# One bias product less for each batch, degrees by reductions, and another order on GpSimd, in a graph network with LSTM windows

## The chip, the cores and the metric

The kernel runs on one core of a Trainium2 chip. The metric is the device time of the launch in microseconds, the median of three runs. Profiles give one execution.

## The reference, cut to what matters

Sixteen batches b of a 512x128 matrix x, and one 512x512 matrix adj for all of them:

```
h = relu(layernorm(x))
h = relu(adj @ (h @ Wg0 + bg0))
h = relu(adj @ (h @ Wg1 + bg1))
for p in 1..4:                        # windows of p tokens
    h[:, p-1::p] = last hidden state of LSTM p over each window of p tokens
x = x + h
h = relu(layernorm(x))
A = adj + I
deg = sum(A, axis=0) + sum(A, axis=1) - diag(A)
A_hat = A * deg[:,None]**-0.5 * deg[None,:]**-0.5
z = relu(batchnorm((A_hat @ h) @ W1.T + b1));  z = batchnorm(z @ W2.T + b2)
out = x + z
```

Both batch norms take their statistics over all batches and tokens.

## The kernel before, in words

Features lie on the partitions, the 512 tokens of a batch in the free axis. Each matrix product in fp32 accuracy is made as three products of split operands (hi x hi, hi x lo, lo x hi, lines 1093 to 1095). The hi part of a tile is a copy by ScalarE in the type fp32r, and the lo part, what is left, is made by VectorE (lines 754 and 756), for some LSTM inputs by GpSimd (line 390). So each step of the first layers runs through TensorE (into a PSUM bank), ScalarE (hi) and VectorE (lo).

The first two layers of a batch are four units. AGG0 multiplies the normed x by adj. LIN0 multiplies by Wg0; since adj @ (h @ Wg0 + bg0) = (adj @ h) @ Wg0 + rowsum(adj) x bg0, it first puts the outer product of bg0 and the row sums of adj into the bank (line 1149, 512 columns), and ScalarE makes h1 by a relu that reads the bank (line 597). It has no lo part. LIN1 (lines 1152 and 1154) reads h1, AGG1 multiplies by adj again.

The main loop has four rounds of 22 slots. A slot is one step of an LSTM on one of two chains: slots 0 to 3 are p = 1, 4 to 7 p = 2, 8 to 13 p = 3, 14 to 21 p = 4. TensorE makes the gates into one of six banks, ScalarE the sigmoids and tanhs (line 641, three instructions; the tanh of the cell at line 651), VectorE the cell and state (lines 925 to 957). Beside it run, by fixed slot numbers, the units of the next four batches (PRE_POS: LIN0 at slots 1, 10, 14 and 19, LIN1 one slot later) and the second network of the batches of the round before (POST_POS). The units of the first four batches stand in the prologue, in an order written out by hand (PROLOGUE), between the banks of weights that are transposed and split. Every engine walks the same lists and works in order. For VectorE a slot is: the LSTM step, then the units' lo parts, then statistics and norms, then what belongs to the matrix A_hat. For ScalarE the relu of LIN0 comes ahead of the next slot's gates.

GpSimd makes in each slot the norms (line 361 to 371) that are due, and the lo parts that the following steps of p = 3 and p = 4 read (line 390).

A_hat is made in round 0. DEG_SUM (slot 3) is 16 products on TensorE that sum rows and columns of adj over all partitions (lines 1201, 1203, 1205), less the diagonal, which VectorE takes out in the prologue (lines 831 and 836). VectorE then takes the partition's own entry out (line 885) and sums (line 889), GpSimd takes the power -0.5 (slot 4, line 405), VectorE builds diagonal blocks of it (DINV_DIAG, slot 5, line 895), TensorE spreads them (DINV_ROWS, slot 7), and VectorE makes four chunks of A_hat (HAT_CHUNK, slots 8, 11, 14, 17; lines 867 to 876 and a lo part).

Of the kernel before, what the change touches and what calls it, by code (L numbers as in the profile page):

```python
# [139 lines left out]
def build(nc, x, adj, Wg0, bg0, Wg1, bg1, Wih, Whh, bih, bhh, W1, b1, g1, be1, W2, b2, g2, be2, out):  # L140
# [7 lines left out]
    with whole:  # L148
# [22 lines left out]
        bg0_row = sb("bg0_row", [P, P], F32R)  # L171
        rowsum_row = sb("rowsum_row", [P, T], F32R)
# [7 lines left out]
        deg = sb("deg", [P, CHUNKS])  # L180
# [57 lines left out]
        def f32(ap):  # L238
# [12 lines left out]
        fix_part, fix_ready, deg_mm, deg_part, deg_ready = (  # L251
            sem("fix_part"), sem("fix_ready"), sem("deg_mm"), sem("deg_part"), sem("deg_ready"))
# [9 lines left out]
        pre_mm, pre_hi, pre_lo, h1_ready = sem("pre_mm"), sem("pre_hi"), sem("pre_lo"), sem("h1_ready")  # L262
# [81 lines left out]
        def _(pool):  # L344
# [8 lines left out]
            nc.gpsimd.memset(f32(bg0_row[:, :]), 0.0)  # L353
# [31 lines left out]

            def later_class(r, chain, q, c):
# [5 lines left out]
            for slot in range(N_SLOTS):  # L392
# [3 lines left out]
                for kind, n in PRE_AFTER[slot]:  # L396
                    if kind == "stats":
                        norm_pre(n)
                for kind, n in POST_AFTER[slot]:
                    if kind == "stats":  # L400
                        norm_post(n, y_post)
                if slot == DEG_POW:

                    pool.wait_ge(deg_ready, 1)
                    nc.gpsimd.tensor_tensor(dinv[:, :], deg[:, :], minus_half[:, :], ALU.pow).then_inc(dinv_ready, 1)
# [947 lines left out]
```

## Time and profile before

| what | value |
|---|---|
| median of three runs | 567.07 us (564.61 to 568.53) |
| the profiled execution | 565.18 us, its span 563.4 us |
| mean granted clock of TensorE | 0.973 of full speed |
| busy: TensorE, VectorE, ScalarE, GpSimd | 90%, 73%, 63%, 35% of the span |
| the chain of work that ended last: TensorE, issue, VectorE, GpSimd, ScalarE | 49%, 21%, 12%, 9%, 5% |

The busy share is an average over the prologue (to about 51 us), four rounds (to about 480 us) and the two batch norms at the end. The timeline gives for each instruction its start and length, and in brackets the time for which its engine was idle before it and what released it. A mean granted clock under 1 in a stretch says that TensorE ran part of it at 1.2 and not at 2.4 GHz.

### The profile page before, as it was taken

How to read it: one execution, taken by the hardware profiler on the slowest of the kernel's cores; microseconds unless marked ns; L12 is line 12 of the kernel's file. 1: busy time of each engine (PE TensorE's matmuls, PEld its weight loads, DVE VectorE, ACT ScalarE, POOL GpSimd, SP SyncE). 2: the span in 40 equal slices, each digit the busy share in tenths (PEclk: the TensorE clock that was granted, in tenths of full speed). 3: DMA queues.
4: the chain of work that ended last, by engine and by line, in shares of the span. 5: the costliest groups of instructions: out<-in, count | busy, mean ns of one | idle time of the engine just before them, and what ended most of it. 6: DMA issues, size and time to landing. Idle time of an engine off the chain costs nothing.

```text
span 563.4 us, 7993 instructions
## 1 busy us (share of the span) xinstructions
PE 504.7 (90%) x2697; PEld 430.3 (76%) x2697; DVE 413.8 (73%) x957; ACT 353.2 (63%) x679; POOL 197.3 (35%) x299
## 2 busy tenths in 40 slices
PE   3998998797898999999989999999779998895866
PEld 3787787797897789988977889889557998673546
DVE  3646667788857888678578887775786888877867
ACT  3544765555567667566676575675766677456863
POOL 4502021304400647055005471440052514247940
PEclk9998999798999999999999999999999999997997
DMA  7300030000001011102011101010910000600007
GB/s 224 114 19 2 0 94 19 2 19 1 19 20 58 37 38 56 58 1 75 31 65 56 37 38 57 2 56 1 366 64 19 20 2 19 224 1 0 1 1 298
DMA packets 17837, 31.21 MB, mean 55 GB/s; under 512 B 1498, under 2 KB 6020, under 8 KB 17796
## 3 DMA queue, kind: packets, MB, share of 16 engines
q1 hardware_dynamic: 16804, 30.17, 15.7%
q10 hardware_dynamic: 992, 0.52, 0.4%
q8 instruction: 21, 0.34, 0.3%
q14 instruction: 20, 0.16, 0.1%
HBM read 19.16 MB, written 11.53 MB: 54 GB/s over the span
## 4 chain that ended last, share of the span: by engine, by line
PE 49%; issue 21%; DVE 12%; POOL 9%; ACT 5%; POOLq 3%; DMA 1%; DVEq 0%; ACTq 0%
PE gate_ps L1093 10%; PE gate_ps L1095 9%; PE gate_ps L1094 9%; PE pre_ps L1094 3%; PE pre_ps L1095 3%; PE pre_ps L1093 3%; POOL x_pre L371 3%; PE post_ps L1093 3%; POOL z_back L426 3%; PE post_ps L1095 2%; PE post_ps L1094 2%; POOLq L369 2%; ACT gate L651 2%; DVE cell L935 1%; PE pre_ps L1154 1%
## 5 line engine op out<-in xcount | busy, mean ns | idle before, releaser
L641 ACT ACTIVATE gate<-gate_ps,gate_bias 128x256 f32<-128x256 f32 (+2 forms) x312 | 164.0, 562 | 45.4 <-PE gate_ps L1095 43.8
L1093 PE MATMUL gate_ps<-by_class_hi,wih_hi 128*128 128x256 f32 (+2 forms) x264 | 86.5, 328 | 15.3 <-POOL by_class_lo L390 9.2
L651 ACT ACTIVATE gate<-cell 128x512 f32<-128x512 f32 (+2 forms) x88 | 45.3, 515 | 68.5 <-DVE cell L930 34.8
L1095 PE MATMUL gate_ps<-by_class_lo,wih_hi 128*128 128x256 f32 (+2 forms) x264 | 84.5, 320 | 0.0
L1094 PE MATMUL gate_ps<-by_class_hi,wih_lo 128*128 128x256 f32 (+2 forms) x264 | 84.4, 320 | 0.0
L1093 PEld LDWEIGHTS gate_ps<-by_class_hi,wih_hi 128*128 128x128 f32 x264 | 50.7, 192 | 22.9 <-POOL by_class_lo L390 10.7
L1093 PE MATMUL gate_ps<-hstep_hi,whh_hi 128*128 128x256 f32 (+2 forms) x192 | 60.7, 316 | 0.0
L1095 PE MATMUL gate_ps<-hstep_lo,whh_hi 128*128 128x256 f32 (+2 forms) x192 | 60.5, 315 | 0.0
L1094 PE MATMUL gate_ps<-hstep_hi,whh_lo 128*128 128x256 f32 (+2 forms) x192 | 60.5, 315 | 0.0
L390 POOL TENSOR_TENSOR by_class_lo<-h,by_class_hi 128x256 fp32r<-128x256 f32 (+1 forms) x40 | 36.8, 927 | 55.4 <-ACT by_class_hi L649 55.3
L1094 PEld LDWEIGHTS gate_ps<-by_class_hi,wih_lo 128*128 128x128 f32 x264 | 50.8, 192 | 3.5
L361 POOL TENSOR_TENSOR ln_pre<-mv_pre,eps 128x4 f32<-128x4 f32 x16 | 5.0, 314 | 137.5 <-DVE mv_pre L802 137.5
L1095 PEld LDWEIGHTS gate_ps<-by_class_lo,wih_hi 128*128 128x128 f32 x264 | 50.6, 192 | 2.3
L361 POOL TENSOR_TENSOR ln_post<-mv_post,eps 128x4 f32<-128x4 f32 x16 | 6.4, 403 | 130.4 <-DVE mv_post L802 130.4
L940 DVE TENSOR_TENSOR gate<-gate 128x256 f32<-128x256 f32 (+2 forms) x48 | 27.3, 569 | 26.3 <-ACT gate L651 26.3
L1094 PEld LDWEIGHTS gate_ps<-hstep_hi,whh_lo 128*128 128x128 f32 x192 | 37.2, 194 | 1.3
L1093 PEld LDWEIGHTS gate_ps<-hstep_hi,whh_hi 128*128 128x128 f32 x192 | 37.1, 193 | 1.3
L1095 PEld LDWEIGHTS gate_ps<-hstep_lo,whh_hi 128*128 128x128 f32 x192 | 37.0, 193 | 1.3
L371 POOL TENSOR_SCALAR x_pre<-x_pre,ln_pre 128x128 f32<-128x128 f32 x64 | 34.9, 557 | 2.8 <-issue 2.8
L371 POOL TENSOR_SCALAR y_post<-x,ln_post 128x128 f32<-128x128 f32 x52 | 33.5, 655 | 2.3 <-issue 2.3
L927 DVE TENSOR_TENSOR gate<-gate 128x256 f32<-128x256 f32 (+2 forms) x48 | 24.3, 506 | 12.5 <-ACT gate L641 12.3
L935 DVE TENSOR_TENSOR cell<-gate 128x512 f32<-128x512 f32 (+2 forms) x40 | 25.6, 640 | 7.3 <-ACT gate L641 7.1
(295 smaller groups left out, 1304.3 us busy)
## 6 DMA issues: line engine op xcount, KB each, us to landing
x_pre<-in_x SPq DMA_DIRECT2D x16, 256.0 KB, 2.7
x<-in_x SPq DMA_DIRECT2D x16, 256.0 KB, 2.7
z_spill<-z_ring SPq DMA_DIRECT2D x8, 512.0 KB, 2.7
z_back<-z_spill SPq DMA_DIRECT2D x8, 512.0 KB, 6.7
x_spill<-x SPq DMA_DIRECT2D x12, 256.0 KB, 2.0
x_back<-x_spill SPq DMA_DIRECT2D x1, 3072.0 KB, 11.2
out<-x_back SPq DMA_DIRECT2D x12, 256.0 KB, 2.3
x<-in_adj SPq DMA_DIRECT2D x1, 1024.0 KB, 6.4
```

Of the source, the lines that this page charges most:

```text
L361: nc.gpsimd.tensor_tensor(ln[:, 0, :], mv[:, :, 1], eps[:, :], ALU.add)
L371: last = nc.gpsimd.tensor_scalar(y[:, c * P:(c + 1) * P], src[:, c * P:(c + 1) * P], ln[:, 2, c:c + 1], ln[:, 1, c:c + 1], ALU.add, ALU.mult)
L390: nc.gpsimd.tensor_tensor(lo, states, f32(hi), ALU.subtract).then_inc(later_lo, 1)
L426: nc.gpsimd.tensor_scalar(zz, zz, bn1[:, 4, half:half + 1], bn1[:, 5, half:half + 1], ALU.mult, ALU.add).then_inc(t_pool, 1)
L641: nc.scalar.activation(gate[:, tile_of(g), gt, 0:size], gate_ps[k % GATE_BANKS][:, 0:size], ACT.Tanh if gt == G_GATE else ACT.Sigmoid, bia ...
L651: nc.scalar.activation(gate[:, tile_of(g), G_GATE, 0:size], cell[:, tile_of(g), 0:size], ACT.Tanh)\
L927: nc.vector.tensor_tensor(i_, i_, g_, ALU.mult).then_inc(ig_done, 1)
L935: nc.vector.tensor_tensor(c_, i_, g_, ALU.mult).then_inc(cell_ready, 1)
L940: nc.vector.tensor_tensor(i_, o_, g_, ALU.mult).then_inc(h_done, 1)
L1093: nc.tensor.matmul(ps, w[0], m[0], start=start, stop=False)
L1094: nc.tensor.matmul(ps, w[1], m[0], start=False, stop=False)
L1095: return nc.tensor.matmul(ps, w[0], m[1], start=False, stop=stop)
```

## The change

**The bias of LIN0.** The outer product at line 1149 is left out. In the prologue a 512-column matrix bias0 is made once: ScalarE copies the row sums of adj, which a bank holds on all partitions, and VectorE multiplies them by bg0, one value to a partition. For every batch VectorE adds bias0 to the bank and writes h1 (both inputs are read with a step of four elements, h1 is written densely); ScalarE then makes the relu in place in h1. There are sixteen such adds, four of them in the prologue.

**The degrees.** The 16 products of slot 3, their two followers on VectorE and one of the two diagonal operations leave. VectorE makes four reductions in the prologue: the rows of adj (in the raw matrix), the hi and the lo part of the transposed adj, and the diagonal. So that a partition holds the same tokens in both, adj is loaded with four consecutive rows to a partition, and the transposes write every fourth column. GpSimd adds the four sums and takes the power ahead of the main loop. DINV_DIAG moves from slot 5 to 2, DINV_ROWS from 7 to 4, the chunks from slots 8, 11, 14, 17 to 5, 9, 12, 17. SyncE's loads of x1 wait for the reductions and not for the products.

**GpSimd's order.** In a slot whose successor makes lo parts, the norms due in it are made one slot later on GpSimd, behind those lo parts. The prologue's second statistics also move behind bank 0 and the first norm.

```diff
-DEG_SUM, DEG_TOKENS, DEG_POW, DINV_DIAG, DINV_ROWS = 3, 3, 4, 5, 7
-HAT_CHUNK = (8, 11, 14, 17)
+DINV_DIAG, DINV_ROWS = 2, 4
+HAT_CHUNK = (5, 9, 12, 17)
+def makes_parts(slot):
+    return slot < N_SLOTS and TURNS[slot][2] >= 3 and TURNS[slot][3] + 1 < TURNS[slot][2]
+NORMS_AFTER = [[at for at in (slot - 1, slot) if at >= 0 and makes_parts(at + 1) == (at < slot)] for slot in range(N_SLOTS)]
...
 PROLOGUE
-        [("stats", 0), ("stats", 1), ("bank", 0), ("norm", 0), ...
+        [("stats", 0), ("bank", 0), ("norm", 0), ("stats", 1), ...
...
-                     ("bank", 7), (LIN1, 0), (LIN1, 1), (LIN0, 2), ("bank", 8), (AGG0, 3), (AGG1, 0), ("bank", 9),
-                     (LIN0, 3), (LIN1, 2), (AGG1, 1), ("bank", 10)]
+                     ("bank", 7), (LIN1, 0), (LIN1, 1), (LIN0, 2), ("bank", 8), ("deg", DEG_ROWS), (AGG0, 3), ("deg", DEG_HI), (AGG1, 0), ("bank", 9),
+                     (LIN0, 3), (LIN1, 2), ("deg", DEG_LO), (AGG1, 1), ("bank", 10)]
...
-                    + [(LIN1, 3), ("bank", 11), (AGG1, 2), ("bank", 12)]
+                    + [(LIN1, 3), ("bank", 11), ("deg", DEG_DIAG), (AGG1, 2), ("bank", 12)]
...
 GpSimd
+            pool.wait_ge(deg_ready, 4)
+            nc.gpsimd.tensor_tensor(deg[:, DEG_ROWS, :], deg[:, DEG_ROWS, :], deg[:, DEG_HI, :], ALU.add)
...
+            nc.gpsimd.tensor_tensor(dinv[:, :], deg[:, DEG_ROWS, :], minus_half[:, :], ALU.pow).then_inc(dinv_ready, 1)
...
+                for at in NORMS_AFTER[slot]:
+                    for kind, n in PRE_AFTER[at]:
...
 SyncE
-            sp.dma_start(adj_raw[:, :, :], adj.rearrange("(c p) s -> p c s", p=P)).then_inc(adj_in, 16)
+            sp.dma_start(adj_raw[:, :, :], adj.rearrange("(p c) s -> p c s", c=CHUNKS)).then_inc(adj_in, 16)
...
-                    sp.wait_ge(deg_mm, 1)
+                    sp.wait_ge(deg_ready, 4)
...
 ScalarE
-                    last = nc.scalar.activation(rowsum_row[:, :], ps[:, :], ACT.Copy)
+                    last = nc.scalar.activation(bias0[:, :], ps[:, :], ACT.Copy)
...
+                if k == LIN0:
+                    act.wait_ge(h1_sum, b + 1)
+                    nc.scalar.activation(h1[i][:, :, :], h1[i][:, :, :], ACT.Relu).then_inc(h1_ready, 1)
+                    return
                 act.wait_ge(pre_mm, q + 1)
-                if k == LIN0:
-                    nc.scalar.activation(h1[i][:, :, :], ps[:, :].rearrange("h (p c) -> h c p", c=CHUNKS), ACT.Relu)\
...
 VectorE
+                    last = nc.vector.tensor_scalar(bias0[:, :], bias0[:, :], bg0_col[:, 0:1], None, ALU.mult)
...
+                if k == LIN0:
...
+                    dve.wait_ge(pre_mm, pre_number(b, k) + 1)
+                    nc.vector.tensor_tensor(h1[i][:, :, :], ps[:, :].rearrange("h (p c) -> h c p", c=CHUNKS),
+                                            bias0[:, :].rearrange("h (p c) -> h c p", c=CHUNKS), ALU.add).then_inc(h1_sum, 1)
+                    return
...
+            def deg_part(i):
+                if i == DEG_DIAG:
...
+                        last = nc.vector.tensor_tensor(deg_fix[:, c, :], adj_raw[:, c, c::CHUNKS], ident[:, :], ALU.mult)
...
+                src = {DEG_ROWS: adj_raw, DEG_HI: adj_t[0], DEG_LO: adj_t[1], DEG_DIAG: deg_fix}[i][:, :, :]
...
+                nc.vector.reduce_sum(deg[:, i, :], src, AX.X).then_inc(deg_ready, 1)
...
 TensorE
-                        last = nc.tensor.transpose(ps[:, c * P:(c + 1) * P], adj_raw[:, c, i::CHUNKS], ident[:, :])
+                        last = nc.tensor.transpose(ps[:, c::CHUNKS], adj_raw[:, c, i::CHUNKS], ident[:, :])
...
-                    nc.tensor.matmul(ps[:, :], bg0_row[:, :], rowsum_row[:, :], start=True, stop=False)
-                    last = product(ps[:, :], [part[:, :] for part in wg0], [part[:, :] for part in agg[i]], False, True)
+                    last = product(ps[:, :], [part[:, :] for part in wg0], [part[:, :] for part in agg[i]], True, True)
...
-                if n == DEG_SUM:
-                    for c in range(CHUNKS):
-                        nc.tensor.matmul(post_ps[:, :], ones_f[:, :], adj_raw[:, c, :], start=c == 0, stop=False)
-                        for part in adj_t:
-                            nc.tensor.matmul(post_ps[:, :], ones_r[:, :], part[:, c, :], start=False, stop=False)
...
```

How VectorE's instructions stand in the prologue, before, around the lo part of the third aggregated batch (agg_lo) and the second linear unit's u_lo:

```order
L756 TENSOR_TENSOR wih_lo<-gate_ps,wih_hi 128x512
L756 TENSOR_TENSOR agg_lo<-gate_ps,agg_hi 128x512
L754 SCALAR_TENSOR_TENSOR lstm_in_lo<-pre_ps,lstm_in_hi 128x512
L756 TENSOR_TENSOR wih_lo<-gate_ps,wih_hi 128x512
L756 TENSOR_TENSOR u_0_lo<-gate_ps,u_0_hi 128x512
```

And the same place in the changed kernel:

```order
L837 TENSOR_TENSOR h_0<-gate_ps,bias 128x512
L771 TENSOR_TENSOR wih_lo<-gate_ps,wih_hi 128x512
L859 TENSOR_REDUCE deg<-x 128x4
L771 TENSOR_TENSOR agg_lo<-gate_ps,agg_hi 128x512
L859 TENSOR_REDUCE deg<-adj_t_hi 128x4
L769 SCALAR_TENSOR_TENSOR lstm_in_lo<-pre_ps,lstm_in_hi 128x512
L771 TENSOR_TENSOR wih_lo<-gate_ps,wih_hi 128x512
L837 TENSOR_TENSOR h_1<-gate_ps,bias 128x512
L771 TENSOR_TENSOR u_0_lo<-gate_ps,u_0_hi 128x512
L859 TENSOR_REDUCE deg<-adj_t_lo 128x4
```

Two adds of bias0 (h_0 and h_1) and three reductions stand between the lo parts that were neighbours.

VectorE in slot 1 of round 0, before (two state products of p = 1, then the hi and lo part of the state), and what follows is the next slot:

```order
L935 TENSOR_TENSOR cell<-gate 128x512
L948 TENSOR_TENSOR cell<-gate 128x512
L950 CAST by_class_hi<-cell 128x512
L756 TENSOR_TENSOR by_class_lo<-cell,by_class_hi 128x512
L935 TENSOR_TENSOR cell<-gate 128x512
```

The same slot in the changed kernel:

```order
L952 TENSOR_TENSOR cell<-gate 128x512
L965 TENSOR_TENSOR cell<-gate 128x512
L967 CAST by_class_hi<-cell 128x512
L771 TENSOR_TENSOR by_class_lo<-cell,by_class_hi 128x512
L837 TENSOR_TENSOR h_0<-pre_ps,bias 128x512
L952 TENSOR_TENSOR cell<-gate 128x512
```

The add stands behind the slot's lo part. On ScalarE the relu of h_0 keeps its place, between the tanh (line 666) and the even tokens (line 675), and reads h_0 where it read the bank.

GpSimd around slots 6 to 9 of round 0, before: the norm of a batch (lines 361 to 371) and the lo parts for p = 3.

```order
L361 TENSOR_TENSOR ln_pre<-mv_pre,eps 128x4
L362 TENSOR_TENSOR ln_pre<-mv_pre,minus_one 128x4
L364 TENSOR_TENSOR ln_pre<-ln_pre,minus_half 128x4
L371 TENSOR_SCALAR x_pre<-x_pre,ln_pre 128x128 x4
L390 TENSOR_TENSOR by_class_lo<-h,by_class_hi 128x340 x4
```

The same place in the changed kernel:

```order
L409 TENSOR_TENSOR by_class_lo<-h,by_class_hi 128x340
L369 TENSOR_TENSOR ln_pre<-mv_pre,eps 128x4
L370 TENSOR_TENSOR ln_pre<-mv_pre,minus_one 128x4
L372 TENSOR_TENSOR ln_pre<-ln_pre,minus_half 128x4
L379 TENSOR_SCALAR x_pre<-x_pre,ln_pre 128x128 x4
L409 TENSOR_TENSOR by_class_lo<-h,by_class_hi 128x340 x3
```

The first of the four lo parts now stands ahead of the norm.

## Rows read from the trace of the kernel before

**Rows 1.** The page: busy us, share of the span and instruction counts of each engine.

```profile
PE 504.7 (90%) x2697; PEld 430.3 (76%) x2697; DVE 413.8 (73%) x957; ACT 353.2 (63%) x679; POOL 197.3 (35%) x299
```

**Rows 2.** Busy by stretch: PE, PEld, DVE, ACT, POOL; PEclk, DMA, GB/s.

```profile
12.00:51.00 39.00, 36.63 (x189) 30.04 (x189) 23.31 (x62) 19.55 (x46) 12.91 (x26) 1.00 0.22 62
66.00:72.40 6.40, 6.40 (x27) 4.05 (x26) 4.68 (x8) 3.77 (x7) 0.00 (x0) 1.00 0.00 0
97.00:103.00 6.00, 1.11 (x5) 0.83 (x5) 5.24 (x10) 2.67 (x6) 5.68 (x9) 0.74 0.00 0
...
181.00:277.00 96.00, 93.84 (x533) 83.02 (x534) 74.41 (x190) 62.44 (x128) 44.23 (x66) 1.00 0.12 42
```

**Rows 3.** Timeline: start us, us, engine, line, op, tiles, shapes, count, idle before.

```profile
102.17 0.65 PE L1093 MATMUL gate_ps<-by_class_hi,wih_hi 128*128 128x340 f32 x1 [4.89 <-POOL by_class_lo L390]
...
134.62 0.58 PE L1093 MATMUL gate_ps<-by_class_hi,wih_hi 128*128 128x256 f32 x1 [2.38 <-POOL by_class_lo L390]
...
469.15 0.38 PE L1093 MATMUL gate_ps<-by_class_hi,wih_hi 128*128 128x256 f32 x1 [1.91 <-POOL by_class_lo L390]
```

**Rows 4.** The chain that ended last, round 1: start us, us, what.

```profile
171.39 1.33 ACT gate L641 x2
...
181.88 0.23 PE gate_ps L1093
```

**Rows 5.** VectorE's groups by shape: busy us, mean ns, then idle before.

```profile
L754 DVE SCALAR_TENSOR_TENSOR hid_lo<-z_back,hid_hi 128x1024 fp32r<-128x1024 f32 x9 | 11.2, 1247 | 3.5 <-ACT hid_hi L733 3.5
...
L870 DVE TENSOR_TENSOR z_ring<-z_ring,ident 128x128 f32<-128x128 f32 x4 | 1.8, 440 | 0.1
```

**Rows 6.** Timeline, slots 1 and 2 of round 0.

```profile
62.57 0.67 ACT L660 ACTIVATE h<-cell 128x256 f32<-128x256 f32 x1 [0.27 <-DVE cell L948]
...
63.04 0.69 DVE L756 TENSOR_TENSOR by_class_lo<-cell,by_class_hi 128x512 fp32r<-128x512 f32 x1
63.05 1.80 ACT L641 ACTIVATE gate<-gate_ps,gate_bias 128x512 f32<-128x512 f32 x3
```

**Rows 7.** Timeline, round 0, slots 3 to 6.

```profile
72.66 0.88 DVE L885 TENSOR_TENSOR z_ring<-post_ps,ident 128x128 f32<-128x128 f32 x4 [1.11 <-PE post_ps L1205]
...
73.34 2.07 ACT L641 ACTIVATE gate<-gate_ps,gate_bias 128x512 f32<-128x512 f32 x3 [2.29 <-PE gate_ps L1095]
...
85.47 0.88 DVE L895 TENSOR_SCALAR z_ring<-ident,dinv 128x128 f32<-128x128 f32 x4 [2.19 <-POOL dinv L405]
```

**Rows 8.** Timeline of the prologue, VectorE and TensorE.

```profile
33.97 0.69 DVE L756 TENSOR_TENSOR agg_lo<-gate_ps,agg_hi 128x512 fp32r<-128x512 f32 x1 [2.00 <-ACT agg_hi L601]
...
51.54 0.50 PE L1093 MATMUL gate_ps<-lstm_in_hi,wih_hi 128*128 128x512 f32 x1 [1.87 <-DVE w_lo L756]
```

**Rows 9.** Timeline, slots 8 to 11 of round 0.

```profile
98.67 0.51 DVE L756 TENSOR_TENSOR hstep_lo<-gate,hstep_hi 128x340 fp32r<-128x340 f32 x1
...
99.70 0.77 DVE L867 TENSOR_TENSOR z_ring<-adj_t_hi,adj_t_lo 128x512 f32<-128x512 f32 x1
...
103.65 0.50 DVE L935 TENSOR_TENSOR cell<-gate 128x340 f32<-128x340 f32 x1
...
106.05 0.51 DVE L925 TENSOR_TENSOR cell<-gate,cell 128x340 f32<-128x340 f32 x1
...
111.45 0.68 DVE L754 SCALAR_TENSOR_TENSOR nrm_lo<-x_pre,nrm_hi 128x512 fp32r<-128x512 f32 x1
...
112.72 0.40 PE L1152 MATMUL pre_ps<-bg_row,ones_r 128*128 128x512 f32 x1
```

**Rows 10.** Timeline, round 0, slots 14 and 19.

```profile
130.23 0.58 ACT L597 ACTIVATE h<-pre_ps 128x512 f32<-128x512 f32 x1
...
131.49 0.68 DVE L867 TENSOR_TENSOR z_ring<-adj_t_hi,adj_t_lo 128x512 f32<-128x512 f32 x1
...
157.89 0.42 DVE L925 TENSOR_TENSOR cell<-gate,cell 128x256 f32<-128x256 f32 x1
...
158.49 0.39 PE L1152 MATMUL pre_ps<-bg_row,ones_r 128*128 128x512 f32 x1
```

More of the change, by code:

```diff
@@ L395, in _ @@
                     later_class(r, chain, p, step + 1)
[L396 to L405, printed above, removed]
+                for at in NORMS_AFTER[slot]:
+                    for kind, n in PRE_AFTER[at]:
+                        if kind == "stats":
+                            norm_pre(n)
+                    for kind, n in POST_AFTER[at]:
+                        if kind == "stats":
+                            norm_post(n, y_post)
             for n in range(LATE, LATE + 2):
@@ L552, in rows_hi_parts @@
                     nc.scalar.activation(wg1[:, :], wg_raw[:, 1, :], ACT.Copy).then_inc(wg_hi, 1)
+                else:
                     act.wait_ge(bias_in, 32)
-                    for row in (0, 32, 64):
-                        last = nc.scalar.activation(bg0_row[row:row + 1, :], bias_rows[row:row + 1, 0, :], ACT.Copy)
-                else:
                     for row in (0, 32):
@@ L560, in rows_hi_parts @@
                                                         bias_rows[row:row + 1, 1, :], ACT.Copy)
-                last.then_inc(rows_hi, 1)
+                    last.then_inc(rows_hi, 1)
             def bank_hi(k):
@@ L769, in rows_lo_parts @@
                         last = low(part, bias_rows[32:33, 1, :], part)
-                last.then_inc(rows_ready, 1)
+                    last.then_inc(rows_ready, 1)
             def bank_lo(k):
@@ L821, in pre_unit @@
                 low(dst[1], src, dst[0], relu=func == ACT.Relu).then_inc(pre_lo, 1)
+            def deg_part(i):
+                if i == DEG_DIAG:
+                    dve.wait_ge(consts_ready, 3)
+                    for c in range(CHUNKS):
+                        last = nc.vector.tensor_tensor(deg_fix[:, c, :], adj_raw[:, c, c::CHUNKS], ident[:, :], ALU.mult)
+                    last.then_inc(diag_part, 1)
+                    dve.wait_ge(diag_part, 1)
+                if i == DEG_HI:
+                    dve.wait_ge(setup_hi, CHUNKS)
+                if i == DEG_LO:
+                    dve.wait_ge(setup_lo, CHUNKS)
+                src = {DEG_ROWS: adj_raw, DEG_HI: adj_t[0], DEG_LO: adj_t[1], DEG_DIAG: deg_fix}[i][:, :, :]
+                if i in (DEG_HI, DEG_LO):
+                    src = f32(src)
+                nc.vector.reduce_sum(deg[:, i, :], src, AX.X).then_inc(deg_ready, 1)
             for kind, i in PROLOGUE:
@@ L825, in _ @@
                     bank_lo(i)
[L826 to L838 removed]
+                elif kind == "deg":
+                    deg_part(i)
                 elif kind == "rows":
@@ L1164, in _ @@
                     bank(i)
-                elif kind not in ("stats", "norm", "rows"):
+                elif kind not in ("stats", "norm", "rows", "deg"):
                     if kind == LIN0 and i == 0:
-                        pe.wait_ge(setup_lo, CHUNKS + 1)
                         pe.wait_ge(wg_ready, 1)
+                    if kind == LIN1 and i == 0:
                         pe.wait_ge(rows_ready, 1)
-                    if kind == LIN1 and i == 0:
-                        pe.wait_ge(rows_ready, 2)
                     pre_unit(kind, i, prologue_ps(i), i % 2)
```

71 lines of the change are left out of this document (24 added, 47 removed).

## The prediction

> **What bounds the kernel now.** I read the page first, then the busy time by stretch, then the chain that ended last, then the timeline around each place that the change touches. The page makes TensorE the fullest engine, 90% busy, and VectorE the next with 73% [rows 1]. The stretches say where that holds [rows 2]: in the round from 181 to 277 us TensorE computes 93.84 of 96 us, but in the prologue (12 to 51 us) it has 2.4 us to spare and VectorE 15.7 us. The timeline has three places at which TensorE idles for a lo part that GpSimd makes, 4.89 + 2.38 + 1.91 = 9.2 us in all [rows 3]. The chain shows that in the four short slots that open a round (p = 1) the limit is not TensorE's products but the alternation of ScalarE's gates and VectorE's state products; rows 4 hold the first such piece of round 1 and the TensorE piece with which it ends. So there are three regimes: TensorE in the middle of a round, the chain of ScalarE and VectorE at its start, and a prologue in which the engines hand each other tiles.
>
> The sum is made against the profiled execution, 565.2 us (its span is 563.4). It lies 1.9 us under the median of the three runs, 567.07.
>
> **Prices.** A 512-column product costs TensorE 0.23 us [rows 4]. The bias product of the first linear layer is one such; there are sixteen. The new add of VectorE reads a PSUM tile and the kept matrix, 128x512 each, both with neighbours 16 bytes apart, and writes h1 densely. The nearest row with that step in SBUF is the identity added to every fourth column: 440 ns for 128 elements, on average [rows 5]. The four products that read PSUM at that step took 0.88 us [rows 7], 0.22 each, so the step in PSUM costs nothing. The identity's add runs partly beside GpSimd, so of its excess of 0.22 over those I give the step about half, 0.12 us per 128 elements. It has the step on its read and on its write, the new add on one SBUF read. A dense 128x512 operation of VectorE takes 0.69 us [rows 6]. The ends are therefore 0.69 and 0.69 + 4 x 0.12 = 1.17, and I take the middle, 0.93, as one of the two steps is there. The relu in place I take at its old 0.58 [rows 10].
>
> The Trainium skill, "SBUF — State Buffer", Door 1, says that accesses keep the full rate only while at least two fall on each 16-byte line, and that PSUM's lines are 8 bytes, so that non-contiguous PSUM patterns slow matmuls. By the first half the add would cost the upper end, and the sum below would be 1.9 us higher. By the second half the adjacency transposes, which now write every fourth column, would be slower than before; the dense price of rows 7 for a PSUM read at that step does not show it, and no row here shows it for that transpose.
>
> A reduction over 2048 elements: I count it by what it reads, as a dense operation of VectorE: 512 take 0.69 [rows 6], 1024 take 1.25 [rows 5], so 0.56 for each further 512 and 2.4 in all. Three of them are 7.1, the diagonal 0.88 + 0.69 = 1.6, the four adds of the prologue 3.7, less 0.3 for a bias row: 12.1 us on a VectorE with 15.7 idle.
>
> **Prologue: +3.1.** VectorE's idle time comes in pieces of 2.0 us, each before a tile that TensorE wants next [rows 8]. Walking the new order: the relu of batch 0 stands ahead of nrm_hi of batch 2 on ScalarE and now waits for VectorE's add; that delays the third aggregation by about 1.2 (0.93, and what stands ahead of the add). Reductions of 2.4 us in gaps of 2.0 leave 0.4 each, 1.2. The diagonal block stands near the end, where nothing hides it, 1.6. Against them stand four bias products, 0.9. 1.2 + 1.2 + 1.6 - 0.9 = 3.1. Ends: -0.9, if all is hidden, and +6.0, if half of the 12.1 is exposed. Stats of batch 1 behind the first lo parts let aggregation 0 start sooner, but aggregation 1 waits for batch 1 as before: nothing.
>
> **Slot 1 of round 0: +2.7.** VectorE's state tail comes first in its queue and the add behind it. The lo part starts at 63.04 and frees the engine 0.61 later, the add takes 0.93, the relu 0.58: h1 is ready at 65.2 [rows 6]. ScalarE waits in order: its even tokens come behind the relu, the gates of slot 2 another 0.48 on (62.57 to 63.05), at 65.7 and not at 63.05, 2.65 later.
>
> **Slots 2 to 8: -1.4.** The degree products fill TensorE for 6.3 of the 6.4 us from 66.0 [rows 2]. What that costs the chain is ScalarE's wait before the next gates, 2.29 us at 73.34 [rows 7]. Without the products ScalarE and VectorE set the pace, so I count 2.3 and not 6.3. DINV_DIAG moves to slot 2 and puts 0.9 on the same chain. Its old wait and itself, 2.19 + 0.88 = 3.1 [rows 7], are replaced by the first hat chunk, which is 4.0 beside GpSimd [rows 9] and which I put at 3.1 without it: even. -2.3 + 0.9 = -1.4.
>
> **Slots 8 to 11: -1.6.** Before 102.17 the lo part waits behind a norm. Taken first it is ready before 97, and the hidden state decides: 98.67 + 0.51 = 99.18, a gain of 3.0 [rows 3, 9]. The granted clock is 0.74 from 97 to 103, so part of that stretch at 1.2 GHz [rows 2], and the product behind the pause takes 0.65 us for 340 columns [rows 3], where 512 take 0.39 at 158.49 [rows 10]. Six such at 0.3 too much are 1.8. Some two microseconds of idling remain, so I credit half, 0.9. But the second hat chunk moves from slot 11 to slot 9, ahead of slot 10's states, and takes 4.0 (99.70 to 103.65). Those states and their tail take 5.4 (106.05 to 111.45), of which 2.0 are waits that the chunk uses up [rows 9]. So VectorE is through slot 9 at 106.05 - 3.9 = 102.15, through the chunk at 106.1, through slot 10 at 109.5, and add and relu end at 111.1, where TensorE asked for h1 at 112.72: 1.6 is left of the 3.9.
>
> **Slots 14 and 19 of round 0: +0.7.** The wait of 2.38 at 134.62 goes [rows 3], but the add can start only at the end of VectorE's tail, 131.49, so the relu ends at 133.00 and not at 130.81; TensorE ran until 132.24, 1.43 behind the relu, and would until 134.4: -0.2. At slot 19 the tail ends at 157.89, the relu at 159.40, and TensorE asks at 158.49 [rows 10]: +0.9. The three bias products of slots 10 to 19 gain nothing here, as TensorE waits.
>
> **Rounds 1 and 2: +3.9.** Slot 1 lies on the chain that ends at 181.88 [rows 4]: +2.65 each. At slots 10, 14 and 19 a slot's products stand between relu and use on a TensorE that is full there [rows 2], so I count no wait; three bias products leave it, -0.7 in each round. 2 x 1.95 = 3.9.
>
> **Round 3: -1.9**, the third wait for GpSimd [rows 3].
>
> Sum: 3.1 + 2.7 - 1.4 - 1.6 + 0.7 + 3.9 - 1.9 = +5.5, and 565.2 + 5.5 = 570.7. GpSimd's norms start up to 1 us later; ScalarE wants them two slots on, nothing. The x loads start earlier behind the degrees, nothing. The adjacency's longer rows lie between -1 and 0; I take 0.
>
> **The rivals.** *TensorE is the bound everywhere.* Then the degree products count in full (6.3), so do sixteen bias products (3.7), the waits for GpSimd down to their next input (3.0, nearly all of 2.38, and 1.91: 6.8 with 1.9 for the second) and the half-rate products (1.8): -18.6, 547; if half is given back at the relu, 556. For it: 93.84 of 96 us. Against it: rows 7, where the neighbour waited only 2.29, and rows 4. Chance of less than 561.4: 0.25. The Trainium skill, "Perfetto Trace Analysis", Identifying the Most-Contended Engine, says to optimise the engine of highest occupancy first; by that rule this rival would be the outcome.
>
> *VectorE has no gap left before the main loop.* Place: the lo parts behind the reductions. If half of the 12.1 us is exposed the prologue costs 6.0 and not 3.1, and an add of 1.17 puts 0.24 on eight exposed places, 1.9: 570.7 + 2.9 + 1.9 = 575.5. It decides once the prologue costs 5.1, or as soon as it costs 3.2 with that add. For it: gaps of 2.0 for pieces of 2.4. Against it: 15.7 us idle. Chance of more than 572.7: 0.33.
>
> *GpSimd's new order does nothing*, since another input is as late: the gains of 1.6, 0.2 and 1.9 fall away, 574.4, and its chance, 0.05, is within the 0.33.
>
> **How the numbers follow.** A measurement of this kernel tells about 1%, 5.7 us, from no change. The forecast lies 3.6 above the median, within it: same 0.42, slower 0.33, faster 0.25. The range from 557 to 578 leaves out 2 in 10: the full gain of TensorE below, a wholly exposed prologue above. The likeliest case alone spans 565 to 573.
>
> **What would show it.** The first gate product moves from 51.54 [rows 8] to about 54.6. The adds last 0.93, the reductions 2.4. In slot 1 of every round ScalarE waits about 2 us for the add, and TensorE for h1 before the second linear layer. The wait at 73.34 is gone, and TensorE has new idle time between slots 4 and 6. No wait on GpSimd's lo part is left at 102 and 469. I am wrong if ScalarE's waits for the add are short, or if the first gate product starts at 51.5 or sooner.

## The result, and the profile after

| | before | changed |
|---|---|---|
| median | 567.04 us (564.61 to 568.53, 4 runs) | 578.67 us (577.85 to 580.92, 4 runs) |
| ratio | | 1.0213, 95% interval 1.0178 to 1.0247 |
| profiled execution, its span | 565.18, 563.4 us | 578.66, 576.9 us |
| mean granted clock | 0.973 | 0.967 |

The change costs 11.6 us, 2.1%. The forecast was 570.7, the range 557 to 578: the sign of the sum was right and the size was not, and the result lies outside. Between the two profiled executions the difference is 13.5 us.

The page of the changed kernel, which answers to [rows 1]: TensorE has lost 32 products (40 records, as each of the eight that read a plain f32 tile stands twice in the trace) and is by this count as busy as before; VectorE has 19.5 us more.

```profile
PE 505.0 (88%) x2657; PEld 428.7 (74%) x2657; DVE 433.3 (75%) x967; ACT 349.0 (60%) x676; POOL 191.3 (33%) x302
```

VectorE's new instructions, grouped by shape (busy us, mean ns, idle before); below, ScalarE's relu from the page, with the idle time ahead of it:

```profile
L837 DVE TENSOR_TENSOR h<-pre_ps,bias 128x512 f32<-128x512 f32 x13 | 13.7, 1054 | 0.0
...
L859 DVE TENSOR_REDUCE deg<-x 128x4 f32<-128x2048 f32 x1 | 2.3, 2275 | 0.0
```

```profile
L612 ACT ACTIVATE h<-h 128x512 f32<-128x512 f32 x16 | 10.1, 631 | 41.0 <-DVE h L837 41.0
```

The add takes 1.05 us (the sum had 0.93, ends 0.69 and 1.17), a reduction 2.28 (2.4), the relu in place 0.63 (0.58). The last row is the important one: in sixteen places ScalarE stood for 41.0 us in all before a relu, waiting for the add.

Slot 1 of round 0, timeline, which answers to [rows 6]:

```profile
65.11 0.69 DVE L771 TENSOR_TENSOR by_class_lo<-cell,by_class_hi 128x512 fp32r<-128x512 f32 x1
65.72 1.04 DVE L837 TENSOR_TENSOR h<-pre_ps,bias 128x512 f32<-128x512 f32 x1
66.79 0.63 ACT L612 ACTIVATE h<-h 128x512 f32<-128x512 f32 x1 [2.91 <-DVE h L837]
67.33 0.64 ACT L675 ACTIVATE h<-cell 128x256 f32<-128x256 f32 x1
67.48 0.54 PE L1167 MATMUL pre_ps<-bg_row,ones_r 128*128 128x512 f32 x1 [2.42 <-ACT h L612]
67.77 1.79 ACT L656 ACTIVATE gate<-gate_ps,gate_bias 128x512 f32<-128x512 f32 x3
```

Lo part, add, relu, even tokens and gates run one behind the other, as forecast. ScalarE waited 2.91 us, TensorE 2.42 for h1.

A simple way to place the loss is to take one event that each slot has, ScalarE's tanh of the cell (88 in a run), and to subtract its start before from its start after. By stretches, in us, for the profiled executions (the columns on the right belong to experiments below: without the bias part; with the add moved):

| stretch, to the tanh of | forecast | changed | without bias | add early |
|---|---|---|---|---|
| prologue, slot 0 | +3.1 | +2.5 | -2.0 | +4.0 |
| slots 1 and 2 | +2.7 | +2.2 | -0.4 | 0.0 |
| slots 3 to 8 | -1.4 | -2.1 | -2.1 | -2.1 |
| slots 9 to 21 of round 0 | -0.9 | +1.2 | -6.6 | -5.2 |
| rounds 1 and 2 | +3.9 | +7.5 | +0.4 | -0.7 |
| round 3 | -1.9 | +2.4 | +2.6 | +1.2 |
| sum | +5.5 | +13.8 | -8.1 | -2.8 |

Up to the end of round 0 the forecast holds in sum (+3.5 against +3.8). It is lost in rounds 1 and 2 (3.6) and in round 3 (4.3). In rounds 1 and 2 the step behind slot 1 is +2.65 and +2.66; most of the rest comes at slot 10. There, in round 1, the changed kernel's timeline shows on VectorE and ScalarE:

```profile
225.54 0.47 ACT L666 ACTIVATE gate<-cell 128x340 f32<-128x340 f32 x1
226.04 0.96 DVE L957 TENSOR_TENSOR gate<-gate 128x340 f32<-128x340 f32 x1 [0.61 <-ACT gate L666]
...
227.87 1.07 DVE L837 TENSOR_TENSOR h<-pre_ps,bias 128x512 f32<-128x512 f32 x1
...
228.97 0.63 ACT L612 ACTIVATE h<-h 128x512 f32<-128x512 f32 x1 [2.96 <-DVE h L837]
...
230.60 1.84 ACT L656 ACTIVATE gate<-gate_ps,gate_bias 128x340 f32<-128x340 f32 x4
...
233.20 0.49 ACT L666 ACTIVATE gate<-cell 128x340 f32<-128x340 f32 x1 [0.35 <-DVE cell L947]
```

and the kernel before, at the same place, had

```profile
219.60 0.49 ACT L651 ACTIVATE gate<-cell 128x340 f32<-128x340 f32 x1 [0.47 <-DVE cell L930]
220.00 0.58 ACT L597 ACTIVATE h<-pre_ps 128x512 f32<-128x512 f32 x1
...
221.57 1.56 ACT L641 ACTIVATE gate<-gate_ps,gate_bias 128x340 f32<-128x340 f32 x3
...
224.36 0.49 ACT L651 ACTIVATE gate<-cell 128x340 f32<-128x340 f32 x1
```

Before, 4.76 us lie from tanh to tanh (219.60 to 224.36); now 7.66 (225.54 to 233.20). The add is behind VectorE's tail, the relu behind the add, and all of the next slot's gates stand behind the relu on ScalarE. TensorE, which I had looked at, goes on with gate products it has banks for and hardly waits; the chain of ScalarE and VectorE is what slips. Not all of the 2.9 us are the add's: without the bias part this step still grows by 0.6, and so it does with GpSimd's order alone. VectorE's product at 226.04 takes 0.96 beside a lo part of GpSimd, where it took 0.51 before. Of the 2.9 us 1.8 are made good in the two slots that follow, and slot 14 adds 0.8.

### The profile page after: what moved, and what is told of

The parts are those of the page before. It is cut to its first block, busy times and chain, and to the rows that moved or that the text cites. A ratio compares the mean times of both kernels' runs of the same rounds, so it can differ in the third digit from the quotient of the medians.

```text
span 576.9 us, 7923 instructions
## 1 busy us (share of the span) xinstructions
PE 505.0 (88%) x2657; PEld 428.7 (74%) x2657; DVE 433.3 (75%) x967; ACT 349.0 (60%) x676; POOL 191.3 (33%) x302
## 4 chain that ended last, share of the span: by engine, by line
PE 36%; DVE 31%; issue 12%; ACT 11%; POOL 6%; POOLq 2%; DVEq 1%; DMA 1%; ACTq 0%
PE gate_ps L1109 7%; PE gate_ps L1111 7%; PE gate_ps L1110 7%; ACT gate L666 4%; ACT gate L656 3%; POOL z_back L443 3%; PE pre_ps L1109 3%; DVE gate L957 2%; PE pre_ps L1111 2%; PE pre_ps L1110 2%; DVE cell L952 2%; DVE hstep_lo L771 2%; DVE cell L947 2%; PE post_ps L1109 2%; DVE gate L944 2%
## 5 line engine op out<-in xcount | busy, mean ns | idle before, releaser
L656 ACT ACTIVATE gate<-gate_ps,gate_bias 128x256 f32<-128x256 f32 (+2 forms) x312 | 160.8, 563 | 34.3 <-PE gate_ps L1111 32.8
L409 POOL TENSOR_TENSOR by_class_lo<-h,by_class_hi 128x256 fp32r<-128x256 f32 (+1 forms) x40 | 35.1, 877 | 160.6 <-ACT by_class_hi L664 160.6
L1109 PEld LDWEIGHTS gate_ps<-by_class_hi,wih_hi 128*128 128x128 f32 x264 | 51.2, 194 | 19.5 <-issue 11.5
L957 DVE TENSOR_TENSOR gate<-gate 128x256 f32<-128x256 f32 (+2 forms) x48 | 28.0, 584 | 26.5 <-ACT gate L666 26.5
L612 ACT ACTIVATE h<-h 128x512 f32<-128x512 f32 x16 | 10.1, 631 | 41.0 <-DVE h L837 41.0
L379 POOL TENSOR_SCALAR x_pre<-x_pre,ln_pre 128x128 f32<-128x128 f32 x64 | 33.5, 535 | 2.8 <-issue 2.8
L944 DVE TENSOR_TENSOR gate<-gate 128x256 f32<-128x256 f32 (+2 forms) x48 | 25.5, 531 | 9.8 <-ACT gate L656 9.7
L379 POOL TENSOR_SCALAR y_post<-x,ln_post 128x128 f32<-128x128 f32 x52 | 31.7, 621 | 2.3 <-issue 2.3
```

The lines of the kernel that those rows point to most:

```text
L379: last = nc.gpsimd.tensor_scalar(y[:, c * P:(c + 1) * P], src[:, c * P:(c + 1) * P], ln[:, 2, c:c + 1], ln[:, 1, c:c + 1], ALU.add, ALU.mult)
L409: nc.gpsimd.tensor_tensor(lo, states, f32(hi), ALU.subtract).then_inc(later_lo, 1)
L656: nc.scalar.activation(gate[:, tile_of(g), gt, 0:size], gate_ps[k % GATE_BANKS][:, 0:size], ACT.Tanh if gt == G_GATE else ACT.Sigmoid, bia ...
L944: nc.vector.tensor_tensor(i_, i_, g_, ALU.mult).then_inc(ig_done, 1)
L957: nc.vector.tensor_tensor(i_, o_, g_, ALU.mult).then_inc(h_done, 1)
L1109: nc.tensor.matmul(ps, w[0], m[0], start=start, stop=False)
```

## The experiments

Each was timed beside the kernel before on the same chip (566.5 to 566.9 us there).

### One part alone, and all but one

The four edits are: the bias part on the kernel before; the degrees part on it; GpSimd's order on it; and the changed kernel with the bias part taken back. For example the last:

```diff
-                    last = product(ps[:, :], [part[:, :] for part in wg0], [part[:, :] for part in agg[i]], True, True)
+                    nc.tensor.matmul(ps[:, :], bg0_row[:, :], rowsum_row[:, :], start=True, stop=False)
+                    last = product(ps[:, :], [part[:, :] for part in wg0], [part[:, :] for part in agg[i]], False, True)
```

> The kernel before with the bias part alone: VectorE adds the kept matrix, ScalarE makes the relu in place; degrees and GpSimd's order as before. If the add on the way to h1 is the cause, slot 1 of rounds 0 to 2 gives +2.65 each (8.0), slots 10, 14 and 19 some +1.5 in each round, and the prologue nothing or +1: 567 + 12 = 579. If the degree reductions carry the loss, this kernel loses at most half of the 11.6 us: 573 or less.

> The degrees part alone (reductions on VectorE in the prologue, hat chunks earlier, statistics of batch 1 later), bias product on TensorE and GpSimd's order as before. If the add is the cause: the prologue costs +2.5 and slot 4 gives 2.7 back, 567 within 2. If the reductions are the cause: 573 or more.

> GpSimd's order alone: lo parts ahead of the norms. In the changed kernel slot 9 of round 0 came 3.9 us sooner and lost it in slots 10 and 11 behind the add; without the add it should keep 2 to 3 us of it, and the waits at slot 14 of round 0 and slot 17 of round 3 give up to 1 each: 563 to 565. A rival: the later norms give it back, 567.

> The changed kernel with the bias product back on TensorE and the relu back on the bank; degrees on VectorE and GpSimd's new order stay. If the add is the cause: 562 to 566, at or under the kernel before. If the reductions are: 572 or more.

| kernel | us | ratio to before, 95% |
|---|---|---|
| bias alone | 582.95 | 1.0245 to 1.0321 |
| degrees alone | 565.75 | 0.994 to 1.000 |
| GpSimd's order alone | 566.47 | 0.9981 to 1.0015 |
| degrees and order, no bias | 558.28 | 0.9817 to 0.9884 |

The bias part is the whole loss: +16.4 us alone, and +20.4 on top of the other two, which without it are 8.2 us faster than the kernel before. My expectation for the bias alone (579) was 4 too low, and 562 to 566 for the kernel without it was 4 too high. The degrees alone came as expected (565.75 for 567 within 2). GpSimd's order alone was expected at 563 to 565 and gives nothing in the time. In its trace it gains 3.0 us in slots 9 to 21 of round 0 and gives back 0.9 in rounds 1 and 2 and 1.05 in round 3; what else its profile loses is 1.4 in the prologue, whose program is unchanged, and 1.6 at slots 6 and 7 of round 3, behind a fall of the granted clock.

Degrees and order together are worth far more than the two alone (-0.8 and 0). By slots, the two alone sum to +0.2 and together make -8.1. Of the 8.3 us, 4.5 lie in round 3, where the profiles of the single parts had falls of the granted clock (below), 2.3 in slots 9 to 21 of round 0, mostly at slot 16, where the kernel with the early chunks and GpSimd's old order loses 2.7 again (TensorE waits 2.35 for GpSimd's lo part at 130.24), and 1.6 in the prologue, which GpSimd's order does not touch: that much two profiles can differ for no reason. So the size of this interplay is measured, its parts are only placed.

### The add's place, its length, and the relu's place

Add moved ahead of VectorE's wait for the tanh, in slot 1 alone, or everywhere (then without the condition):

```diff
+                if p == 1:
+                    for kind, n in PRE_AFTER[g]:
+                        if kind == LIN0:
+                            pre_unit(kind, n, pre_ps, 0)
                 dve.wait_ge(tanh_ready, g + 1)
```

Kept matrix stored in h1's order:

```diff
-                    last = nc.scalar.activation(bias0[:, :], ps[:, :], ACT.Copy)
+                    last = nc.scalar.activation(bias0[:, :].rearrange("h (c p) -> h c p", c=CHUNKS),
+                                                ps[:, :].rearrange("h (p c) -> h c p", c=CHUNKS), ACT.Copy)
```

For the late relu, the call moves on ScalarE from the end of slot g to behind the gates of slot g + 1.

> The changed kernel with the add of slot 1 moved on VectorE: behind the cell's product and ahead of the wait for the tanh, where VectorE idles 0.7 us. If the 2.65 us per round are the add's place behind the state's tail, slot 1 costs at most 0.6 and three rounds give back 6: 572.5. If they are the longer way itself (add and relu one behind the other, wherever they stand), 577 or more.

> The changed kernel with the kept matrix stored in h1's order, so that the add reads it densely and only the bank with a step. If the step in SBUF makes the add 1.05 us and not 0.69, the add falls to 0.7 and, on 10 to 13 exposed places, the kernel to 574.5. If the step in PSUM is what costs, the add stays at 1.05 and the time at 578.

> The changed kernel with ScalarE's relu of LIN0 behind the next slot's gates, not ahead of them: ScalarE no longer stands before the add, TensorE still waits for h1 before the second linear layer. If ScalarE's wait in its queue is the cost, slots 1 and 10 give back most of what they lose: 568 to 572. If TensorE's wait for h1 is, the time stays at 577 or more, as the relu comes still later.

> The changed kernel with the add ahead of the wait for the tanh in every slot that has one, the kept matrix read with its step as before (1.05 us). Moved in slot 1 alone it gave 6 us, moved everywhere and dense 18.5. If slots 10, 14 and 19 lose by the add's place, this kernel comes to 563 to 565; if the shorter add is what mends them, to 570.

> The changed kernel with both mendings: the dense kept matrix (3 us) and the add ahead of the wait for the tanh, in slots 10, 14 and 19 too. The slot-1 move gave 6 us; in the other slots the add now delays the state by up to 0.4 but lets the relu end some 0.9 sooner. Sum 578.7 - 3 - 6 - 1 = 569. If the longer slots suffer from the delayed state, 572.

| kernel | us | against the changed kernel |
|---|---|---|
| add early in slot 1 | 572.65 | -6.0 |
| add early in every slot | 561.78 | -16.9 |
| dense kept matrix | 575.6 | -3.1 |
| add early everywhere, and dense | 560.18 | -18.5 |
| relu late | 585.17 | +6.5 |

The add's place is the cause. Early, it uses the time in which VectorE waits for the tanh; timeline of slot 1 of round 0 with the add early in slot 1:

```profile
63.43 0.69 DVE L952 TENSOR_TENSOR cell<-gate 128x512 f32<-128x512 f32 x1 [0.89 <-ACT gate L656]
64.04 1.07 DVE L837 TENSOR_TENSOR h<-pre_ps,bias 128x512 f32<-128x512 f32 x1
64.16 0.63 ACT L666 ACTIVATE gate<-cell 128x512 f32<-128x512 f32 x1 [0.18 <-DVE cell L952]
65.02 0.69 DVE L969 TENSOR_TENSOR cell<-gate 128x512 f32<-128x512 f32 x1
65.14 0.63 ACT L612 ACTIVATE h<-h 128x512 f32<-128x512 f32 x1 [0.35 <-DVE h L837]
```

The add delays the state's product by 0.2 us, ScalarE waits 0.35 instead of 2.91. In slot 10 of round 1, with the add early everywhere, the relu follows the tanh after 0.43 of idling:

```profile
215.78 1.08 DVE L837 TENSOR_TENSOR h<-pre_ps,bias 128x512 f32<-128x512 f32 x1
...
215.96 0.50 ACT L666 ACTIVATE gate<-cell 128x340 f32<-128x340 f32 x1
...
216.90 0.64 ACT L612 ACTIVATE h<-h 128x512 f32<-128x512 f32 x1 [0.43 <-DVE h L837]
```

With the add early everywhere ScalarE's waits for it sum to 16.1 us, not 41.0. Against my doubt about the longer slots, the moved place helped there too: slots 10, 14 and 19 were worth 10.9 us beside slot 1's 6.0. Against the kernel with slot 1 alone moved, the tanh behind slot 10 comes 2.0 to 2.4 us sooner in each round and the one behind slot 14 1.3 to 1.6; the one behind slot 19 comes 1.7 sooner in round 0 and no sooner in rounds 1 and 2, where the changed kernel had lost nothing there. The late relu was the wrong remedy: ScalarE's waits for the adds fell from 41.0 to 12.1 us, but TensorE's waits for h1 rose from 13.5 to 21.2. Against what was expected, the two single mendings came out (572.65 for 572.5, 575.6 for 574.5), the add early everywhere did better (561.78 for 563 to 565; with the dense matrix, which was run first, 560.18 for 569), and the late relu did the opposite (585.17 for 568 to 572).

The length counts less. One row of the kernel with the dense matrix (ns min/median/max, first and last start):

```profile
L838 DVE TENSOR_TENSOR h<-pre_ps,bias x13: 681/683/685, 20.3 to 390.8; 128x512 f32<-128x512 f32 x13
```

0.683 us instead of 1.05, although the bank is still read at a step of four. So the step in PSUM costs VectorE nothing, and the one step in SBUF costs 0.37 us for 512 elements, where the sum had taken 0.24. The Trainium skill, "SBUF — State Buffer", Door 1, says that full rate needs two accesses to each 16-byte line; the read that falls on one element of each is this case, and the trace agrees: 1.05 against 0.683. The same page's sentence on PSUM concerns matmuls, and the transposes that now write every fourth column took 417 ns at the median before and 418 after; no slowing shows.

### The prologue

The first four batches without bg0 (the add left out and the relu back on the bank; this part of the computation is missing), and, without the bias part, the second statistics back in front. Then the whole computation, with the bias of the first four batches on TensorE and of the other twelve by the early, dense add:

```diff
+                if k == LIN0 and b < EARLY:
+                    return
                 if k == LIN0:
```

> The changed kernel without bg0 for the first four batches (their relu reads the bank again, the add is left out; a part of the computation is missing). Before the main loop the changed kernel stood 4.5 us behind the kernel without the bias part. If these are the four adds of the prologue on a VectorE that the reductions have filled, it gives back about 4: 574.5. If they come from the reductions themselves, 578.

> The kernel without the bias part and with the old chunk slots, with the prologue's second statistics back in front of bank 0. That kernel reached the first slot 1.9 us sooner than the kernel before, in spite of 9 us of reductions. If the statistics' new place gives this, 559; if the reductions simply lie in VectorE's idle time and the diagonal operation that is gone gives it, 557.4.

> Bias product and relu from the bank for the first four batches, the dense add ahead of the tanh for the other twelve. The prologue's adds cost 4 us (574.8 without them against 578.7), less 1 for the second set of bias rows: 560.2 - 3 = 557. A rival: the added copies of the row sums take it back, 559.

Measured 574.8, 558.5 and 558.03 us. The first gate product of the changed kernel starts at

```profile
55.24 0.50 PE L1109 MATMUL gate_ps<-lstm_in_hi,wih_hi 128*128 128x512 f32 x1 [2.51 <-DVE w_lo L771]
```

and without the four adds at

```profile
50.19 0.50 PE L1116 MATMUL gate_ps<-lstm_in_hi,wih_hi 128*128 128x512 f32 x1 [1.87 <-DVE w_lo L776]
```

against 51.54 before [rows 8]. So beside the reductions the four adds cost 5.05 us of the prologue in the trace and 3.9 in the time. Each part alone costs far less. With degrees and order but no adds the first gate product comes at 50.74, so there the reductions cost nothing; with the bias part alone, adds but no reductions, it comes at 53.29, 1.75 late. One execution tells little here: with GpSimd's order alone, which leaves the prologue's program as it was, it comes at 52.80. But the two together, +3.7, are 2.75 more than the sum of the two alone (+1.75 and -0.8), about twice that spread. The likely reason is that adds and reductions fill the same idle time of VectorE. My +3.1 was near the sum; its parts (reductions 2.8, adds 0.3) no run confirms, as what a part costs depends on whether the other is there: taken off the changed kernel the adds give back 4 to 5 us, the degrees part 1.95. The statistics' place is within the spread (558.5 against 557.4). The mixed kernel came at 558.03 for 557.

### GpSimd's order and the chunks

Without the bias part: the normalized adjacency's steps at their old slots; then also the new order in round 0 alone, or in all rounds but the last.

```diff
-NORMS_AFTER = [[at for at in (slot - 1, slot) if at >= 0 and makes_parts(at + 1) == (at < slot)] for slot in range(N_SLOTS)]
+NORMS_AFTER = [[at for at in (slot - 1, slot) if at >= 0 and (makes_parts(at + 1) and at < 3 * len(ORDER)) == (at < slot)] for slot in range(N_SLOTS)]
```

> The kernel without the bias part (558.3 us) with the steps of the normalized adjacency back at their old slots (diagonal 5, rows 7, chunks 8, 11, 14, 17). If the 8 us come from the chunks' earlier slots, 565; if from the reductions that took 16 products off TensorE, 560 or less.

> The kernel without the bias part and with the old chunk slots (557.4), with GpSimd's new order in round 0 alone. The new order gained some 3 us in slots 9 to 15 of round 0, while rounds 1 to 3 showed +0.3 to +0.7 at slots 11, 12, 16 and 18. If the later norms cost there, this kernel gains 1.5 to 2.5: 555 to 556. If these steps are something else, 557.4.

> The kernel without the bias part and with the old chunk slots (557.4), with GpSimd's new order in rounds 0 to 2 and the old one in round 3. By the sum's last step (the wait of 1.91 us of TensorE at slot 17 goes) this kernel loses 1.9: 559.3. If that wait lay beside the chain of ScalarE and VectorE, the slots from 11 to 19 take 0.7 less here, and what is left is the granted clock behind the wait: 556.7 to 558.5.

> The same with the steps of the normalized adjacency at their old slots. Without the bias part these slots made no difference that could be measured (557.4 and 558.3), though the trace has the old ones 0.2 ahead at the end: 556.5. If the early chunks compete with the adds for VectorE in slots 9 to 12, 555.

Measured 557.41, 559.64, 559.63 and 559.09 us. Two of these miss what was expected: the order in round 0 alone (555 to 556, or 557.4) and the mixed kernel with the old slots (556.5). The 559.63 meets the 559.3 of the sum, but not for the sum's reason, as the traces show below. The chunks' slots do not matter (557.41 against 558.28, and 559.09 against 558.03 the other way). For the order in round 3 two effects have opposite signs. With the old order there (timeline of GpSimd, ScalarE, VectorE and TensorE, slots 17 and 18):

```profile
458.93 1.83 POOL L409 TENSOR_TENSOR by_class_lo<-h,by_class_hi 128x256 fp32r<-128x256 f32 x2
459.28 0.42 ACT L668 ACTIVATE gate<-cell 128x256 f32<-128x256 f32 x1 [0.95 <-DVE cell L943]
459.73 0.43 DVE L953 TENSOR_TENSOR gate<-gate 128x256 f32<-128x256 f32 x1 [0.48 <-ACT gate L668]
459.89 0.39 PE L1106 MATMUL gate_ps<-by_class_hi,wih_hi 128*128 128x256 f32 x1 [1.93 <-POOL by_class_lo L409]
...
462.85 0.42 DVE L940 TENSOR_TENSOR gate<-gate 128x256 f32<-128x256 f32 x1
```

With the new one, in the changed kernel:

```profile
481.67 0.42 ACT L666 ACTIVATE gate<-cell 128x256 f32<-128x256 f32 x1 [0.78 <-DVE cell L947]
481.93 0.73 POOL L409 TENSOR_TENSOR by_class_lo<-h,by_class_hi 128x256 fp32r<-128x256 f32 x1
482.12 0.82 DVE L957 TENSOR_TENSOR gate<-gate 128x256 f32<-128x256 f32 x1 [0.48 <-ACT gate L666]
...
483.83 0.36 PE L1109 MATMUL gate_ps<-by_class_hi,wih_hi 128*128 128x256 f32 x1 [0.82 <-issue]
...
485.06 0.79 POOL L409 TENSOR_TENSOR by_class_lo<-h,by_class_hi 128x256 fp32r<-128x256 f32 x1 [2.40 <-ACT by_class_hi L664]
485.17 0.95 DVE L944 TENSOR_TENSOR gate<-gate 128x256 f32<-128x256 f32 x1
...
486.69 0.42 ACT L666 ACTIVATE gate<-cell 128x256 f32<-128x256 f32 x1 [1.71 <-DVE cell L947]
```

TensorE's wait fell from 1.93 to 0.82 us, but from tanh to tanh it is 5.02 us instead of 4.56. GpSimd's lo parts now run at the same time as VectorE's products of two tiles: these take 0.82 and 0.95 us where they took 0.43 and 0.42. The Trainium skill, "SBUF — State Buffer", Summary: rules for kernel authors, says that an operation of VectorE with two SBUF inputs and a reading one of GpSimd exclude each other, so that the second to start waits. These rows agree, with 0.4 and 0.5 us: both times GpSimd had started first, by 0.2 and 0.1 us. With the old order the product at 459.73 meets GpSimd's two lo parts where one ends and the next begins, and takes 0.43. That order has a price of its own, smaller: VectorE's cast of the state behind that product takes 0.71 beside the second lo part, and 0.29 in the changed kernel. By slots the new order costs 1.1 us net between slots 10 and 19 of round 3, in each profile that has it, and nothing comes back for TensorE's shorter wait, which lay beside the chain.

Yet the kernel with the old order in round 3 is not faster (558.08 to 563.02 us, six runs). At the last tanh its profile stands 1.0 us ahead of the same kernel with the new order in every round (557.41); it is behind it in the first 15 us of what follows that tanh, by 1.9 us. Busy time there, with the clock behind POOL, of the kernel with the old order in round 3 and of that with the new one:

```profile
479.90:486.70 6.80, 6.08 (x15) 4.63 (x15) 5.38 (x24) 2.28 (x5) 3.27 (x7) 0.50 0.59 222
```

```profile
479.70:486.50 6.80, 6.80 (x24) 5.25 (x23) 6.52 (x28) 3.12 (x5) 2.85 (x5) 0.75 0.76 283
```

TensorE ran the first stretch at 1.2 GHz throughout and the second at 1.2 GHz in part. So the granted clock is the likely reason; no run sets it apart from all else. It falls in other places too. Busy time of slots 17 and 18 of round 3, columns as above, of the kernel with the old order in rounds 1 to 3, and of the one with it in round 3 only:

```profile
461.08:467.06 5.98, 5.38 (x32) 5.38 (x33) 3.94 (x8) 3.65 (x8) 1.48 (x2) 0.71 0.14 47
```

```profile
459.28:463.84 4.56, 3.95 (x33) 3.96 (x34) 3.90 (x8) 3.71 (x8) 1.48 (x2) 1.00 0.23 61
```

Behind the same wait of 1.9 us the mean granted clock was 0.71 in the one and full in the other; from tanh to tanh it took 1.4 us more. Five profiles have that wait: bias alone, degrees alone and the order in round 0 had the fall, the kernel before and this one had not; no profile with the new order had it. Slot 6 of round 3 has a fall of its own, behind a wait of TensorE of 2.8 us that the kernel before has too (2.81 at 415.36, 2.83 at 426.73 in the changed one). It costs 1.0 to 2.5 us, and it stands in 14 of the 17 profiles beside that of the kernel before, whatever the order; here the kernel before and the changed one, columns as above:

```profile
415.89:422.35 6.46, 6.46 (x30) 5.36 (x29) 5.51 (x15) 3.80 (x7) 3.39 (x6) 1.00 0.17 43
```

```profile
427.27:434.84 7.57, 7.57 (x30) 6.14 (x29) 5.72 (x15) 4.02 (x7) 4.33 (x8) 0.84 0.11 35
```

## Why the prediction was wrong

**Right.** Slot 1: +2.65 forecast, +2.65 in each of three rounds. That it is so exact is luck: add and relu were 0.12 and 0.05 longer, and the steps between them and the gates as much shorter. Slots 2 to 8: -1.4 against -2.1, the degree products giving back 2.72 where I took 2.3. The waits for GpSimd in round 0 did go (102.17 came at 101.94 with a kernel 2.7 us behind, and 2.0 of idling remain, as forecast). But the gain of 3.9 at slot 9, which the sum took from that wait and from the clock behind it, has another source: the degrees alone show 3.86 at this tanh with the wait still there (4.93 at 97.92), as a chunk of A_hat has left slot 8; without the bias part and with the chunks at their old slots it is 0.6. GpSimd's order alone gains 2.1 in slots 9 to 11. The rival that TensorE is the bound everywhere fell: sixteen degree products and sixteen bias products left it, and the time rose; the degree products alone gave back 2.7 us and not 6.3. The rival of a full VectorE names the right engine, and in the prologue the right place, if only for adds and reductions together. It had no place for the larger loss, in the main loop.

**Wrong, rounds 1 and 2.** The failed step is "At slots 10, 14 and 19 a slot's products stand between relu and use on a TensorE that is full there [rows 2], so I count no wait". It asked only when TensorE wants h1. Who waits first is ScalarE, whose next gates stand behind the relu in its queue; the 2.96 us at 228.97 are that wait. In slot 1 I had asked that question, in slots 10, 14 and 19 not. In rounds 1 and 2 the step to the tanh behind slot 10 grew by 2.9 and 2.2 us and the one behind slot 14 by 0.8 each time; slot 19 lost nothing there. Beside slot 1 the forecast had -1.4 for both rounds; the trace has +7.5 less 5.3 for slot 1, +2.2, of which 0.4 stand without the bias part too. With the add early the two rounds come to -0.7, slot 1 included.

**Wrong, round 3.** "-1.9, the third wait for GpSimd". That an engine waits does not put the wait on the chain. The chain there is ScalarE and VectorE, and the order costs it 1.05 us. The other 1.4 us of the +2.4 go with the fall of the clock at slots 6 and 7 (0.84 against 1.00), which the one profile of the kernel before does not have. It is probably no effect of the change: each part alone shows it, and three kernels that hold parts of the change do not. The times say the same: the profiled execution of the changed kernel lies at its median, that of the kernel before 1.9 us under its own, so of the 13.5 us between the profiles 11.6 are left between the medians.

**Right in sum only.** Round 0 with its prologue, +3.8 for +3.5. The prologue is told above. Slots 9 to 21 came at +1.2 and not at -0.9: the kernel without the bias part gains 6.6 there, and the adds take 7.8. I let each gain end at the next relu; that was right in kind. But up to the tanh of slot 15 the trace has -0.4 where I summed -1.8, and slot 19 costs 1.8 where I had 0.9. There too I had asked only when TensorE wants h1; with the add early slot 19 costs 0.1.

**Open.** Why the clock falls in one execution and not in another; whether the kernel before has the fall at slot 6 in executions that were not profiled; and the exact parts of the interplay of degrees and order, and of adds and reductions.

The versions furthest ahead of both kernels are the change without its bias part (558.28 us, and 557.41 with the old chunk slots) and the one with the mended bias part (558.03): 1.5% under the kernel before (for 558.28 the ratio is 0.985, 95% interval 0.982 to 0.988). Nothing tells them apart, so the bias product may as well stay on TensorE: twelve products fewer bought nothing.

## What to carry to other kernels

When work moves from the fullest engine to another, ask of each engine that works in order what stands behind the new wait in its queue, at every place and not only at the one that looks tight; the consumer of the result may be the last to suffer. Put the moved operation where its new engine already waits: here that was worth 16.9 of 20.4 us, and making it a third shorter only 3.1. A wait that the trace shows is a gain only if the chain runs through it.

## What the runs showed of the hardware

VectorE adds a 128x512 PSUM tile read at a step of 16 bytes to a dense SBUF tile in 0.683 us, and to an SBUF tile read at that step in 1.05. A reduction over 2048 elements took 2.28 us. Two two-input products of 256 columns (0.42 us elsewhere) took 0.82 and 0.95 where a lo part of GpSimd had started 0.1 to 0.2 us before them. Behind one and the same wait of 1.9 us of TensorE the mean granted clock was 0.71 in one profile, a part of the stretch at 1.2 GHz, and full (2.4 GHz) in another, and the stretch took 5.98 and 4.56 us.
